# Two transformer layers on one core: features made in pieces, pairs taken at once, a weight loaded in place, plain rows moved between batches, last rows tile by tile

## The reference

```python
# layer 0: linear attention, then a gated feed-forward with 4-bit weights (1408 wide)
x = _layernorm(x + _L0_attn_ref(...)); x = _layernorm(x + _L0_ffn_ref(...))
# layer 1: gated linear attention in chunks
q = softmax(x @ Wq.T); k = sigmoid(x @ Wk.T); v = x; gf = log_sigmoid(-k)
o = _gla_chunk(q, k, v, gf)
go = o @ Wog.T + x @ Wig.T
on = o * rsqrt(mean(o * o) + EPS) * g_norm_w
x = _layernorm(x + (on * (go * sigmoid(go))) @ Wo.T)
# layer 1: the 512 best of 1024 rows of each batch take a feed-forward (2048 wide)
scores = x @ router_weight + router_bias
top_scores, indices = jax.lax.top_k(scores, K)
h = gelu(x[indices] @ w1 + b1); processed = h @ w2 + b2
x = _layernorm(x.at[indices].add(x[indices] + processed * sigmoid(top_scores)))
```

## Time and profile before

| | |
|---|---|
| median of 3 runs | 1035.98 us (1033.57 to 1036.64) |
| the profiled execution, its own time | 1035.46 us |
| its span | 1033.7 us |
| TensorE busy | 91% |
| VectorE, ScalarE, POOL busy | 65%, 39%, 30% |
| mean granted clock of TensorE, share of full speed | 0.967 |

### The profile page before, as it was taken

How to read it: one execution, slowest core, us unless ns; L and a number is a source line. 1 busy time by engine, 2 the same in 40 slices (tenths; PEclk the granted TensorE clock), 3 DMA queues, 4 the chain that set the end, 5 groups by cost and what they waited for, 6 DMA issues and landing times.

```text
span 1033.7 us, 12330 instructions
## 1 busy us (share of the span) xinstructions
PE 942.8 (91%) x4182; PEld 739.7 (72%) x4182; DVE 671.2 (65%) x1317; ACT 402.6 (39%) x673; POOL 305.0 (30%) x269
## 2 busy tenths in 40 slices
PE   7999999897899999999998988999989789989992
PEld 5777888775577877777766666777857568778882
DVE  4766653677988688688667666657684686463052
ACT  4532122212334543543564564454543263313220
POOL 1000100002576444344333222131224321734332
PEclk9999999999899999999999988999989899989997
DMA  8432100202000000000100110010200343250030
GB/s 285 133 107 87 42 31 31 73 11 57 16 16 11 0 1 1 1 1 1 41 1 1 51 42 1 1 41 1 82 1 22 122 154 110 76 180 11 31 123 41
DMA packets 41790, 52.63 MB, mean 51 GB/s; under 512 B 5888, under 2 KB 23680, under 8 KB 41728
## 3 DMA queue, kind: packets, MB, share of 16 engines
q1 hardware_dynamic: 39904, 47.63, 14.3%
q0 software_dynamic: 1824, 4.22, 1.2%
HBM read 41.33 MB, written 10.50 MB: 50 GB/s over the span
## 4 chain that ended last, share of the span: by engine, by line
PE 44%; DVE 15%; issue 8%; ACT 5%; POOL 3%; DMA 1%; DVEq 0%; ACTq 0%; POOLq 0%
PE ps_gla L41 11%; PE ps_gla L42 10%; PE ps_gla L43 10%; DVE acc L1528 7%; PE ps_gla L2059 5%; PE ps_gla L2060 4%; ACT acc L1255 1%; DVE router_junk L1664 1%; PE ps_gla L2163 1%; POOL p_lo L1898 1%; DVE gsg L1626 1%; PE ps_gla L2094 1%; PE ps_gla L2149 1%; DMA gw_raw<-in_gla_woT 1%; DVE junk L1696 1%
## 5 line engine op out<-in xcount | busy, mean ns | idle before, releaser
L1528 DVE SCALAR_TENSOR_TENSOR acc<-ps_gla,gu_scale,acc 128x512 f32<-128x512 f32 x264 | 196.2, 749 | 66.6 <-ACT acc L1255 45.1
L2059 PE MATMUL ps_gla<-xt_hi,gu_val 128*128 128x512 f32 x352 | 146.9, 417 | 19.3 <-DVE acc L1528 8.5
L2060 PE MATMUL ps_gla<-xt_lo,gu_val 128*128 128x512 f32 x352 | 139.8, 397 | 0.0
L2059 PEld LDWEIGHTS ps_gla<-xt_hi,gu_val 128*128 128x128 f32 x352 | 67.1, 191 | 59.7 <-DVE acc L1528 41.4
L1255 ACT ACTIVATE acc<-ps_gla,gu_scale 128x512 f32<-128x512 f32 x88 | 60.5, 688 | 119.0 <-PE ps_gla L2060 119.0
L1970 POOL TENSOR_TENSOR fsg<-fsg,acc 128x512 f32<-128x512 f32 x44 | 62.1, 1410 | 132.2 <-DVE acc L1528 132.2
L616 POOL TENSOR_TENSOR a_rstd<-a_var,minus_half 128x1 f32<-128x1 f32 x16 | 10.8, 677 | 227.2 <-DVE a_var L508 227.2
L2060 PEld LDWEIGHTS ps_gla<-xt_lo,gu_val 128*128 128x128 f32 x352 | 67.5, 192 | 11.0
L1975 POOL TENSOR_TENSOR fh_lo<-fsg,fh_hi 128x512 fp32r<-128x512 f32 x44 | 56.8, 1291 | 51.9 <-ACT fh_hi L1267 51.9
L41 PE MATMUL ps_gla<-dn_hi,fh_hi 128*128 128x512 f32 x176 | 70.5, 401 | 1.6 <-POOL fh_lo L1975 1.6
L42 PE MATMUL ps_gla<-dn_hi,fh_lo 128*128 128x512 f32 x176 | 69.6, 396 | 0.0
(11 more groups left out here) (267 smaller groups left out, 2229.4 us busy)
## 6 DMA issues: line engine op xcount, KB each, us to landing
mw_raw<-in_w SPq DMA_DIRECT2D x16, 512.0 KB, 3.8
a_nib<-in_gate_up_packed SPq DMA_DIRECT2D x88, 64.0 KB, 2.2
x<-x SPq DMA_DIRECT2D x16, 256.0 KB, 2.5
mw_raw<-x SPq DMA_DIRECT2D x8, 512.0 KB, 4.2
out<-mw_raw SPq DMA_DIRECT2D x8, 512.0 KB, 2.9
xt_raw<-in_xT SPq DMA_DIRECT2D x3, 1024.0 KB, 5.0
x<-in_x SPq DMA_DIRECT2D x3, 1024.0 KB, 6.0
a_nib<-in_down_packed SPq DMA_DIRECT2D x8, 256.0 KB, 3.1
```

Source lines behind the costliest of these rows:

```text
L1528: dve.scalar_tensor_tensor(out=a[:, :], in0=ps[:, FG + c, :], scalar=gu_scale[:, part * IT + j, c:c + 1], in1=a[:, :], op0=ALU.mult, op1=A ...
L2059: pe.matmul(ps[:, FG + c, :], gu_val[:, o, c, :], xt_hi[b % 2][:, c, :], start=True, stop=False)
L2060: pe.matmul(ps[:, FG + c, :], gu_val[:, o, c, :], xt_lo[b % 2][:, c, :], start=False, stop=True).then_inc(s_gu, 1)
```

## The change

- `features(n)` is split into `key_pairs`, `query_pairs`, `query_copies` and `key_copies`; for block 0 they stand before and behind the second groups of steps 8 and 9.
- The 16 transposes of x[1] (`transpose_x(NBLK + 1, c)`) stand ahead of the last down block of layer 0, in the groups' banks, no longer in tiles 0 and 1 of attention block 0; so do their high and low parts.
- `WO` is loaded into the place of its own low half (124 KB) when the last down block is done.
- `take_features` becomes `take_pairs` and `take_queries`. The pairs of tile 0 of the next block are taken before `p_high(n, 3)`; the queries follow it. `project_out` waits for `p_low` chunk by chunk.
- VectorE's order: `router(0)` ahead of `features(2)`; `rank(0, 0)` to `rank(0, 2)` between `gated(2, 2)` and `gated(2, 3)`; in block 3 `variance(2)`, `lower_half(0)` and the low parts of the last two chunks (`last_p_low`, before on POOL) among the `gated`.
- TensorE projects chunks 0 to 2 of two tiles of block 3, then chunk 3 of both.
- Batch 0: six `up` ahead of the first `down`, the scores' broadcast behind the fifth; two pairs of plain rows beside batch 0 (steps 14 and 15), six beside batch 1 (from step 3), the stores of batch 0 from step 9.
- Batch 1: the last two down blocks tile by tile (`last_downs`), and addition, statistics, power, normalisation and store for each tile by itself.

```diff
-        w_raw = [put("gw_qk_raw", [P, KC, P], 192)] + [put("gw_raw", [P, KC, C], 64)] * 3
+        w_raw = [put("gw_qk_raw", [P, KC, P], 192)] + [put("gw_raw", [P, KC, C], 64)] * 2 + [put("gwo_raw", [P, KC, C], 124)]
...
-            if k <= NBLK:
+            if k <= NBLK + 1:
                 return FG + c
-            return (Y, OT, G + 1, Y)[c] if k == NBLK + 1 else G + c % 2
+            return G + c % 2
...
+            sp.wait_ge(s_dn, IT * NBLK)
+            sp.dma_start(w_raw[WO][:, :, :], woT).then_inc(s_w[WO], 16)
             sp.dma_start(rw_sb[:, :], router_w.to_broadcast([P, C])).then_inc(s_rw, 16)
-            sp.wait_ge(s_wl, 3)
-            sp.dma_start(w_raw[WO][:, :, :], woT).then_inc(s_w[WO], 16)
...
-            def take_features(n, t):
+            def take_pairs(n, t):
                 i = TB * n + t
-                act.wait_ge(s_pl, KC * n)
+                if n:
+                    act.wait_ge(s_pl, KC * n - 2)
                 act.activation(pair_t[t % 2][:, :, :].rearrange("d a n -> d (a n)"), ps[0:2 * DK, F, 0:2 * P], ACT.Copy).then_inc(s_pt, 1)
+
+            def take_queries(n, t):
+                i = TB * n + t
+                if n:
+                    act.wait_ge(s_pl, KC * n - 1)
                 act.activation(q_parts[t % 2][:, :], ps[:, F, 2 * P:3 * P], ACT.Copy).then_inc(s_qh, 1)
...
+            for c in range(KC):
+                x_high(NBLK + 1, c)
             act.wait_ge(s_gu, KC * (unit(LAST, IT - 1, 1) + 1))
             weight_high(WIG)
...
-                    take_features(n, t)
-                    if n == 0:
-                        for c in (range(3), range(3, 4), (), ())[t]:
-                            x_high(NBLK + 1, c)
-                    elif n < LAST:
+                    if n == 0 or t:
+                        take_pairs(n, t)
+                    take_queries(n, t)
+                    if 0 < n < LAST:
                         x_high(NBLK + n + 1, t)
...
+                silu(n, 2)
                 if n == 2:
                     take_scores(0, O)
-                silu(n, 2)
                 p_high(n, 2)
                 silu(n, 3)
+                if n < LAST:
+                    take_pairs(n + 1, 0)
                 p_high(n, 3)
...
+                if n:
+                    dve.wait_ge(s_pl, KC * n - 1)
...
+            def last_p_low(m):
+                dve.wait_ge(s_ph, KC * LAST + m + 1)
+                dve.tensor_tensor(p_lo[:, m, :], sg[m][:, :], p_hi[:, m, :].bitcast(F32), ALU.subtract).then_inc(s_pll, 1)
...
+            def finish_selected(t):
+
+                x_ = xsel[1][:, t, :]
+                dve.wait_ge(m_yt, TB + t + 1)
+                dve.wait_ge(m_b2, 3 * TB + t + 1)
+                dve.scalar_tensor_tensor(out=x_, in0=ps[:, MY + t, :], scalar=sel[1][:, t, 1:2], in1=x_, op0=ALU.mult, op1=ALU.add).then_inc(m_r, 1)
+                dve.wait_ge(m_r, TB + t + 1)
+                dve.bn_stats(m_st[:, t, :], x_).then_inc(s_mst, 1)
+                dve.wait_ge(s_mst, TB + t + 1)
+                dve.memset(m_filler[:, :], 0.0)
+                dve.bn_aggr(m_mv[:, t, :], m_st[:, t, :]).then_inc(m_ag, 1)
+                dve.wait_ge(m_ag, TB + t + 1)
+                dve.tensor_scalar(m_var[:, t:t + 1], m_mv[:, t, 1:2], LN_EPS, None, ALU.add).then_inc(m_vr, 1)
+
+            def normalise_selected(t):
+                x_ = xsel[1][:, t, :]
+                dve.wait_ge(m_rs, t + 2)
+                dve.tensor_scalar(x_, x_, m_mv[:, t, 0:1], m_rstd[:, t:t + 1], ALU.subtract, ALU.mult).then_inc(m_out, 1)
...
+                    if b == LAST and j == FRONT_SUMS + 1:
+                        key_pairs(0)
+                    if b == LAST and j == FRONT_SUMS + 2:
+                        query_copies(0)
                     groups(b, j, 1)
...
-                        features(0)
+                        query_pairs(0)
+                    if b == LAST and j == FRONT_SUMS + 2:
+                        key_copies(0)
+            for c in range(KC):
+                x_low(NBLK + 1, c)
             weight_low(WIG)
...
+                if n == 1:
+                    router(0)
                 if n < LAST:
                     features(n + 1)
                 else:
                     rank(0, 7)
                 if n == 0:
                     folded_low(range(2, KC))
-                if n == 2:
-                    rank(0, 0)
-                elif n == 1:
-                    router(0)
                 gated(n, 2)
                 if n == 2:
-                    rank(0, 1)
+                    for t in range(3):
+                        rank(0, t)
+                elif n == LAST:
+                    variance(2)
+                    last_p_low(2)
+                    lower_half(0)
                 gated(n, 3)
-                if n == 2:
-                    rank(0, 2)
-            variance(2)
-            lower_half(0)
+            last_p_low(3)
...
-                for k in range(NPB * b, NPB * (b + 1) + 1):
-                    if k < NPB * (b + 1):
+                first, behind = ((0, PLAIN_0), (PLAIN_0, NPL))[b]
+                for k in range(first, behind + 1):
+                    if k < behind:
                         plain_statistics(k)
-                    if k > NPB * b:
+                    if k > first:
                         plain_normalise(k - 1)
                 selected_residual(b)
                 if b + 1 < NB:
                     selected_low(b + 1)
-                add_outputs(b)
-                layer_norm_block(dve, b, xsel[b], m_st, m_mv, m_var, m_rstd, m_filler, m_r, s_mst, m_ag, m_vr, m_rs, m_out)
+                    add_outputs(b)
+                    layer_norm_block(dve, b, xsel[b], m_st, m_mv, m_var, m_rstd, m_filler, m_r, s_mst, m_ag, m_vr, m_rs, m_out)
+            for t in range(TB):
+                finish_selected(t)
+                if t:
+                    normalise_selected(t - 1)
+            normalise_selected(TB - 1)
...
-                    if PLAIN <= j < PLAIN + NPB:
-                        plain_rstd(j - PLAIN)
+                    if j >= FT - PLAIN_0:
+                        plain_rstd(j - FT + PLAIN_0)
                 else:
                     if j == 2:
-                        selected_rstd(0)
-                    if j == 4:
+                        selected_rstd(slice(0, TB), 0)
+                    if PLAIN <= j < PLAIN + NPL - PLAIN_0:
+                        plain_rstd(PLAIN_0 + j - PLAIN)
+                    if j == STORE:
                         pool.wait_ge(m_out, TB)
                         plain_stored(pool, NPB)
-                    if 4 <= j < 4 + TB:
-                        store_selected(0, j - 4)
-                    if PLAIN <= j < PLAIN + NPB:
-                        plain_rstd(NPB + j - PLAIN)
-
-            PLAIN = 10
+                    if STORE <= j < STORE + TB:
+                        store_selected(0, j - STORE)
+
+            PLAIN = 3
+            STORE = 9
...
-                p_low(n, 2)
-                p_low(n, 3)
+                else:
+                    p_low(n, 2)
+                    p_low(n, 3)
...
-            selected_rstd(1)
             plain_stored(pool, NPL)
             for t in range(TB):
-                pool.wait_ge(m_out, TB + t + 1)
-                store_selected(1, t)
+                selected_rstd(slice(t, t + 1), t + 1)
+                if t:
+                    pool.wait_ge(m_out, TB + t)
+                    store_selected(1, t - 1)
+            pool.wait_ge(m_out, TB + TB)
+            store_selected(1, TB - 1)
...
+            def project_chunks(n, t, chunks_of_c):
+                i = TB * n + t
+                for c in chunks_of_c:
+                    if t == 0:
+                        if n < LAST:
+                            pe.wait_ge(s_pl, KC * n + c + 1)
+                        elif c < 2:
+                            pe.wait_ge(s_pl, KC * LAST + c + 1)
+                        else:
+                            pe.wait_ge(s_pll, c - 1)
+                    ins = three_products(pe, ps[:, y_bank(n, t), :], p_hi[:, c, t * P:(t + 1) * P], p_lo[:, c, t * P:(t + 1) * P],
+                                         w_hi[WO][:, c, :], w_lo[WO][:, c, :], c == 0, c == KC - 1)
+                if c == KC - 1:
+                    ins.then_inc(s_y, 1)
...
+            def last_downs(first):
+
+                for t in range(TB):
+                    for j in range(first, FT):
+                        pe.wait_ge(m_hh, FT + j + 1)
+                        pe.wait_ge(m_hl, FT + j + 1)
+                        n = chunks.index((W2, j // 2))
+                        ins = three_products(pe, ps[:, MY + t, :], h_hi[j % HS][:, t * P:(t + 1) * P], h_lo[j % HS][:, t * P:(t + 1) * P],
+                                             m_hi[n][:, j % 2, :], m_lo[n][:, j % 2, :], False, j == FT - 1)
+                    ins.then_inc(m_yt, 1)
...
-            for k in range(IT * NBLK - 2, IT * NBLK):
-                down_half(k, 0)
```

(26 more changed lines are left out.)

62 lines of the change are left out of this document (31 added, 31 removed).

## The result

| | before | change |
|---|---|---|
| median | 1036.31 us (1033.57 to 1036.66, 4 runs) | 1006.85 us (1005.34 to 1007.95, 4 runs) |
| ratio | | 0.972 (95% interval 0.9699 to 0.9742) |
| the profiled execution: its own time, its span | 1035.46, 1033.7 us | 1005.34, 1003.6 us |
| TensorE busy, mean granted clock | 91%, 0.967 | 93%, 0.986 |

A forecast was written before the change was run, and what follows sets the result against it. TensorE, busy 91%, was taken as the bound, with time in its waits, low clock and the tail. The terms summed to 26.9 us, giving span 1006.8 and time 1008.6 us, 27 below the median; range 1001 to 1019.

The forecast's parts named there:

- Items 7 and 8: Plain rows moved between the batches, gain 6.1 us; last rows finished tile by tile in the tail, gain 3.2 us.
- Item 1: Block 0: features in pieces gain 1.1 us, a wait of 0.5 to 2 staying; with transposes moved ahead, 2.4 us.
- Item 2: End of block 0: output projection weight loaded 20 us earlier shortens the waits for o_lo; gain 0.9 us.
- the term between 0 and 2.4: Possible lateness of WOG if its load shared bandwidth with the output weight's: bounds 0 and 2.4 us, taken as 0.
- Item 3: Pairs taken at once, before the last p_lo: gain 5.2 us from block 0 to 1, 2.5 from block 1 to 2.
- The 0.9 for the mask: Block 0 to 1: a cost of 0.9 us for the mask, after the scores, within the gain of 5.2.
- Item 4: Block 2 to 3: three ranks delay the last product; new waits 2.6, 1.4, 2.0; loss 0.3 us instead of gain 3.0.
- Item 5: End of block 3: projection in chunks and earlier gathers start the first up 9.3 us earlier, 1.7 from the clock.
- Item 6: Five ups before the scores' broadcast: one wait of 4.1 replaces two; gain 0.1 us, with 2.5 charged for low clock.
- the charged clock loss: Low clock expected behind the roughly 4 us wait ahead of up 4, charged at 2.5 us.
- Item 7: Plain rows moved from batch 0 to batch 1: POOL's waits and low clock go; gain 6.1 us, batch 1 losing nothing.
- the clock falls in more places: Rival, 23%: new waits of 1.8 to 2.6 in blocks 1 to 3 bring low clock; 10 us less gain, 1018 us.

The follow-up runs named there:

- the change again: The change itself, unaltered, timed and profiled once more in the later series: 1008.17 us, ratio 0.9752.
- u2: The change with the output projection's weight loaded behind the low half of WOG again, into the new place: 1007.63 us.
- u3: The change with the pairs of tile 0 of blocks 1 to 3 taken behind the last high part again, their shorter semaphore wait kept: 1011.65 us.
- v2: The change with the low half of weight chunk 3 made earlier, between variance and normalisation of block 3: 1002.75 us.
- u5: The change with the last two low parts of block 3 made by POOL again, the projection in chunks kept: 1013.92 us.
- u6: The change with four ups again before the scores' broadcast, then two downs: 1006.93 us.
- u8: The change with the last two downs over all tiles again, then additions, statistics, one power, normalisations and stores of the block: 1010.41 us.
- u7: The change with four pairs of plain rows beside each batch from step 10 again, stores from step 4: 1012.68 us.
- u1: The change with the features of block 0 made in one piece again, the moved transposes of x[1] kept: 1009.03 us.

## Why the prediction was right, point by point

The sum came out (26.9 forecast, 28.6 measured from where the changed code begins), and the base was right: the time came from TensorE's waits and its clock, and from the tail. Items 7 and 8 hit, in the traces and when undone. Elsewhere sizes were off by up to 2.5 us, in both directions, and that only 1.6 of it is left in the sum is partly luck.

- **Item 1** (2.4, measured 3.2). The step "the engine is VectorE-bound there and I take 1.1 us gained" was too low: waits of 0.7 stayed, the lower end of my 0.5 to 2. Undone, the pieces are worth 1.9 for those 1.1.
- **Item 2** (0.9, measured 3.4). The wait itself shrank little: 2.1 and 0.7 became 1.2 and 1.0. What went is 3.4 us lost to low clock behind it, which I had not given to this place. Undone alone it costs 0.5 and no clock. So the forecast's size for the load was about right, and the clock's part was missing here. `WOG` did not land late: it took 5.1 us from its issue (5.2 before), and `WO` behind it 7.3. So the term between 0 and 2.4 was rightly taken as 0.
- **Item 3**, block 0 to 1 (5.2, measured 2.8). The new waits came where I had put them (`k_end` 1.3 for 1.8, `pair_t` 1.5 for 2.0, `p_lo` 0.4 for 0.5). The step that failed is the start: I counted from 613.8 at full clock, so the clock gained ahead of it was booked here and not in item 2. The two together are 6.2 measured, 6.1 forecast. The 0.9 for the mask did not appear. Block 1 to 2 is right in size and mechanism: 1.8 of it because the pairs no longer wait for the last `p_lo`, 0.8 by their place.
- **Item 4** (-0.3, measured 0.9). The mechanism stood, rank 3 ahead of the last product; the waits were 1.9, 1.0 and 0.9 for 2.6, 1.4 and 2.0, and one of 0.6 followed two tiles on. All three terms were too large, the residual's most; with the third rank moved the place gives 1.8 us more.
- **Item 5** (9.3, measured 7.5). The gathers did start as forecast, and they are 6.2 of it when undone. The wait for `xsel` was 2.2 for 1.9. What I left out is low clock behind that wait (785 to 805, 0.91: 1.8 us).
- **Item 6** (-2.4 with the charge, measured -1.3). The wait for the lower half of chunk 3 came, 2.9 for 4.1, and the charged clock loss came with it, 1.7 for 2.5. In the change again the wait was 4.1. The working has a slip here: two waits of 3.0 against 4.1 less 1 give -0.1, not 0.1.
- **Item 7** (6.1, measured 6.1). The working counts 1.8 us over five steps, 9 in all, against 8 in hand, and calls it nothing. In the change the trips took up to 7.5 us, and one low part of batch 1 (951.03) began some 2 us late behind a power; TensorE did not wait for it.

Of the rivals, "the clock falls in more places" stands for what the forecast feared most and saw least: the new waits of 1.2 to 1.9 us had no low clock behind them in this profile, the wait for `xsel` had. Its price was wrong too: in block 3 the low clock cost nothing in the profiles that have it, because VectorE is the later one there. The rule of the Trainium skill that was weighed there (TensorE: Matmul & The Clock Gate, HAM oscillation) ties the fall to idle gaps longer than any of these. This case's runs disagree in part: low clock followed two waits of 1.86 and 0.99 in a row, with 0.72 granted over 6 us in u2.

What stays open: I can't say from these runs why the same wait is followed by low clock in one profile and not in the next, so how much of the 11 us would come back in other executions is known only through the medians, over runs of one kernel that spread by 2 to 4 us. Not undone by themselves were the 16 transposes of item 1, the new wait of `take_pairs` in item 3 and the projection in chunks of item 5, so their shares (for item 5 at most the 1.3 between 7.5 and 6.2) are read from the traces only.

## What to carry to other kernels

Count a wait of the bounding engine together with the low clock that can follow it; here the second was some 11 us beside 14. Before crediting an edit, ask which engine is the bound at the next wait: 1.3 us won at `xsel` came back to 0.2 us ahead of up 4. When a move is undone to price it, undo what it waits for as well as its place: in u3 the first was worth 1.8 us of 2.6. And a queue's order is worth looking at operation by operation: one rank moved behind a product gave 2.0 us, one weight half moved into a pause 4.5.

## What the runs showed of the hardware that was not expected

**Behind the same short waits the clock falls in some profiles and not in others.** With TensorE's code and waits the same, the profiles differ: behind the waits of 1.86 and 0.99 in block 3 the clock stayed up in the change, in its repetition, in v2, u5, u6 and u8, and was low for 3.4 us in u2 and u7 and for 6.8 in u1. A wait of 2.9 for `mw_lo` had it in the change, u5 and u8, and not in u3. In u1 alone waits of 1.2 and 1.0 at the end of block 0 had it (611 to 615). In the kernel before a wait of 2.5, at 694, had none:

```profile
692.00:702.00 10.00, 7.49 (x36) 4.87 (x33) 5.49 (x11) 4.18 (x10) 2.53 (x2) 1.00 0.01 2
```

What it costs is not the same either. Where VectorE is the later one it costs nothing: C and D together are 115.5 us in the change again, u2 and u7 and 115.6 in u1, with 0, 3.4, 3.4 and 6.8 us of low clock at the start of block 3; A is 53.8 in u1 as elsewhere; and of the 1.7 lost behind `xsel` in the change 0.2 is left by the last store. Where TensorE is the later one it is the full 1.7 (stretch E of u3 against the change again: 2.8, of which 1.2 is the shorter wait).

**VectorE's operations on two SBUF operands grow beside POOL.** The forecast had this for `q_pair` (item 1), not for the router. Two products of the router of block 3 in the change, the second beside a `mh_lo` on POOL:

```profile
809.87 0.69 DVE L1697 CUSTOM_DVE_ANT_0 router_junk<-x,rw_sb 128x512 f32<-128x512 f32 x1
...
810.61 1.66 DVE L1697 CUSTOM_DVE_ANT_0 router_junk<-x,rw_sb 128x512 f32<-128x512 f32 x1
```

```profile
810.14 1.58 POOL L2091 TENSOR_TENSOR mh_lo<-mh,mh_hi 128x512 fp32r<-128x512 f32 x1 [2.25 <-ACT mh_hi L1502]
```

The second ends 0.55 us behind POOL's, near the 0.69 that it takes alone. It happens twice in that router, and so it does in the kernel before (832.65 and 835.09, 1.66 each): 2 us on the path to the broadcast, but no part of the difference. New in the change is one such product in block 1's router (672.85, 1.65; before all four took 0.69). The Trainium skill (SBUF — State Buffer, Who interferes with whom) says that a VectorE instruction with two inputs in SBUF contends with a GpSimd instruction that reads SBUF, over a port pair that is locked for one of them. The trace agrees: 0.97 us more.
